# Four graph layers on one core: norms inside their loops, long VectorE operations cut up, the sorted list loaded without a meeting

## The chip, the cores and the metric

The kernel runs on one core of a Trainium2 chip. The core has five engines with a queue each: PE (TensorE), DVE (VectorE), ACT (ScalarE), POOL (GpSimd) and SP (SyncE, which issues transfers). The metric is the device time of one execution in microseconds, lower is better; the time before is the median of three runs.

## The reference

Four graph layers, each on `relu(layernorm(x))`, each added to `x` (3125 nodes of 64 values, 53125 edges with random ends):

```python
# layer 0: sum, maximum and mean of the edges' 32 attributes by source node, then a dense layer
h = jnp.concatenate([seg_sum, seg_max, seg_mean, u[batch]], axis=1)
h = jax.nn.relu(h @ W1 + b1) @ W2 + b2
# layer 1: attention with 8 heads over edges and self loops, softmax by destination node
logits = jax.nn.leaky_relu(a_src[src] + a_dst[dst], negative_slope=0.2)
out = jax.ops.segment_sum(h[src] * alpha[:, :, None], dst, num_segments=n).mean(axis=1) + bias
# layer 2: messages of edge, sender and receiver, mean by destination node, then an update
h = jax.nn.silu(msg_in @ W1_msg + b1_msg)
node_messages = _segment_mean(h @ W2_msg + b2_msg, receivers, node_emb.shape[0])
new = jax.nn.silu(concat([node_emb, node_messages]) @ W1_upd + b1_upd) @ W2_upd + b2_upd
# layer 3: signed cosine similarity of Wh at the two ends, weighted sums by source node
prop_pos = jax.ops.segment_sum((base * sim_pos)[:, None] * Wc, row, num_segments=n_nodes)
```

## The kernel before, in words

Nodes lie in 25 tiles of 128 (`x` and `hn` are 128 partitions x 25 x 64). Each tile group (`GROUPS`) has four tiles, 256 columns of `x`, but for the last, with one tile. A list of 56320 entries (edges, one entry per node, padding) lies as 128 partitions x 440. What a layer needs of its entries' other ends POOL gathers with indirect DMAs, one for each of the 440 columns: 128 rows of a table in HBM. There are five such lists of gathers: the edge records of layer 0 (L838), the edge rows in destination order (L1284, L1303, L1312), and the tables of layers 1, 2 and 3 (L792); and three times 25 gathers for the node sums (L968, L2388, L2761).

`sort_sources` sorts the entries by source node on DVE. Meanwhile PE and ACT make the edge rows of layer 2: 55 units of a product (`project`) and a copy (`keep`), and after each fifth unit ACT issues a store of 1320 KB (L584). When the sort is done, SP stores the keys (L352) and waits, all engines meet (`Step`), SP loads the keys back in another shape (L640), DVE masks the entry's index out of them (L666), and POOL, which waits for `indexed` (L834), begins layer 0's gathers.

While POOL gathers, DVE sorts by destination and makes layer 0's sums. `collect` turns them into node sums: `sel` (L1006) compares 3200 columns at once. POOL's 25 gathers of node sums are followed by early edge gathers (`early_edges`). `layer0_finish` then makes the features, a dense layer in a loop over the groups (`node_dense`: PE transposes, ACT copies, PE, ACT, PE, DVE adds), the norm over all 25 tiles at once (`normalise`), and the table of layer 1, which SP stores; SP raises `renewed` (L1247), for which POOL waits before layer 1's gathers. The bias of layer 1 is added in `layer1_spread` (L1698), that of layer 2 in `layer2_weights` (L2160), each with one operation of 1600 columns.

`layer2_tail` works in a loop over the seven groups, in which the engines' stages are shifted against each other. For a group: the average on DVE (L2541, L2543), transposes on PE (L2429), a copy on ACT (L2491), a product (L2438), DVE's join with the node's own part (L2567), SiLU on ACT (L2498), a second product (L2447), and on DVE the addition to `x` and the centring and squares of the norm (L2549 to L2559), two rounds later. What is carried over from the partition before comes in by products on PE (`carries`, L2413), the third set of them before group 2. After the loop follow one square root, seven norms of two operations each (L2577, L2579), the products for layer 3 (L2460, L2469) and seven pieces of its table on DVE (L2583 to L2588), each stored by two transfers (L2396, L2397). POOL begins layer 3's gathers when all fourteen have landed.

## Time and profile before

| | us |
|---|---|
| median of the three runs (3107.81 to 3112.47) | 3111.59 |
| profiled execution, its own time | 3117.0 |
| span of the profiled execution | 3115.1 |
| POOL busy (71% of the span, 2299 instructions) | 2197.5 |
| DVE busy (42%) | 1320.8 |
| PE busy (20%) | 608.3 |
| ACT busy (15%) | 481.4 |

The shares are of the span. POOL has issue time of 0.30 us between two gathers that doesn't count as busy. Line numbers are those of the kernel before; SPq and ACTq are the transfers that SyncE and ScalarE issue.

### The profile page before, as it was taken

The page shows a single profiled execution, that of the slowest core. Times are in us where ns is not written, and L with a number is a line of the kernel's source. Part 1 is how long each engine was busy: PE and PEld are TensorE (multiplying, and loading weights), DVE is VectorE, ACT ScalarE, POOL GpSimd, SP SyncE. Part 2 cuts the span into 40 slices and gives each one's busy share as a digit, 9 for nine tenths or more (in the row PEclk, how much of TensorE's full clock was granted, in tenths as well). Part 3 has the DMA queues.
Part 4 walks back from the last instruction along what each step waited for, and adds up shares of the span by engine and source line. Part 5 has one row for each costly group of instructions (what it writes and reads, how often), then busy time and mean ns, then how long its engine had stood idle before and what let it go on. Part 6 is the DMA issues. An engine that isn't in the chain of part 4 may idle for free.

```text
span 3115.1 us, 14443 instructions
## 1 busy us (share of the span) xinstructions
PE 608.3 (20%) x3300; PEld 468.3 (15%) x3301; DVE 1320.8 (42%) x1909; ACT 481.4 (15%) x447; POOL 2197.5 (71%) x2299
## 2 busy tenths in 40 slices
PE   5421130001500000001888850000000400000001
PEld 5411110001300000001666640000000300000001
DVE  8788885202310000009466643243344505353455
ACT  2200006211100000000000022222223211211220
POOL 0177777777777777777777777777777367777774
PEclk8665565555555555555899975555555555555555
DMA  9311115212355756755455424333333222323232
GB/s 321 113 25 15 14 27 92 70 33 62 65 52 52 65 59 59 64 52 65 110 135 150 108 51 74 108 90 128 91 117 91 42 55 72 90 72 91 72 88 53
DMA packets 195586, 248.87 MB, mean 80 GB/s; under 512 B 138820, under 2 KB 149694, under 8 KB 187975
## 3 DMA queue, kind: packets, MB, share of 16 engines
q0 software_dynamic: 74048, 114.24, 20.2%
q1 hardware_dynamic: 63414, 104.50, 10.5%
q10 hardware_dynamic: 58064, 29.51, 8.5%
q14 instruction: 45, 0.36, 0.0%
q8 instruction: 15, 0.25, 0.0%
HBM read 154.17 MB, written 93.93 MB: 80 GB/s over the span
## 4 chain that ended last, share of the span: by engine, by line
POOL 55%; issue 19%; DVE 2%; ACT 0%; DMA 0%; DVEq 0%; POOLq 0%; ACTq 0%
POOL l1g_rows L792 13%; POOL l2g_rows L792 13%; POOL l3g_rows L792 12%; POOL ep_rows L1303 11%; POOL ep_rows L1284 2%; POOL l2t_res L2388 1%; POOL l0f_res L968 1%; POOL l3t_res L2761 1%; DVE l3g_banks L2708 0%; DVE l3g_banks L2732 0%; ACT l3g_banks L2666 0%; DVE l3g_banks L2729 0%; DVE l3g_dot L2715 0%; DVEq L2714 0%; POOL ep_rows L1312 0%
## 5 line engine op out<-in xcount | busy, mean ns | idle before, releaser
L838 POOL DMA_INDIRECT l0g_rows<-in_rec_s,ents x440 | 427.3, 971 | 139.8 <-issue 133.8
L792 POOL DMA_INDIRECT l2g_rows<-tab,ep_rows x440 | 417.6, 949 | 134.2 <-issue 134.2
L792 POOL DMA_INDIRECT l1g_rows<-tab,srct x440 | 416.9, 948 | 134.1 <-issue 134.1
L792 POOL DMA_INDIRECT l3g_rows<-tab,others x440 | 416.1, 946 | 134.2 <-issue 134.2
L1303 POOL DMA_INDIRECT ep_rows<-recp,entd x352 | 339.9, 966 | 107.3 <-issue 107.3
L1505 DVE TENSOR_TENSOR l1s_A<-l1s_bank,l1s_mk 110x512 f32<-110x512 f32 x8 | 5.3, 688 | 533.6 <-PE l1s_bank L1467 533.6
L1763 PE MATMUL l1a_pa<-l1a_g,l1a_wt 128*128 x1296 | 169.2, 290 | 0.0
L1763 PEld LDWEIGHTS l1a_pa<-l1a_g,l1a_wt 128*128 128x128 f32 x1296 | 158.7, 202 | 24.3 <-issue 24.3
L2328 DVE COPY l2g_mix<-l2g_q 128x64 f32<-128x64 f32 x11 | 2.5, 228 | 308.1 <-ACT l2g_mix L2289 308.1
L2706 DVE COPY l3g_banks<-l3g_q 128x65 f32<-128x65 f32 x12 | 2.7, 229 | 306.9 <-ACT l3g_banks L2666 306.6
L1467 PE MATMUL l1s_bank<-ident,atp 128*110 128x128 f32 x64 | 11.4, 357 | 544.5 <-ACT atp L1406 535.6
L2767 PE MATMUL l3t_nmp<-ident,l3t_nmb 128*64 128x128 f32 x2 | 0.7, 448 | 585.3 <-DVEq L2784 585.3
L1284 POOL DMA_INDIRECT ep_rows<-recp,entd x82 | 83.2, 1015 | 25.0 <-issue 24.7
L1779 DVE TENSOR_TENSOR l1a_wt<-l1a_place,item_ex 128x1536 f32<-128x1536 f32 x54 | 94.9, 1758 | 7.7
L302 POOL IOTA iot<- 128x3200 f32 x1 | 2.8, 2803 | 132.8 <-DVE sorts_raw L316 132.8
L1406 ACT COPY atp<-l1g_rows 128x704 f32 (+1 forms) x10 | 8.3, 827 | 554.8 <-DMA l1g_rows<-tab,srct 554.8
L1467 PEld LDWEIGHTS l1s_bank<-ident,atp 128*110 128x110 f32 x64 | 10.9, 218 | 545.2 <-issue 536.1
L2666 ACT COPY l3g_banks<-l3g_rows 128x2860 f32<-128x2860 f32 (+3 forms) x12 | 55.2, 4599 | 221.0 <-DMA l3g_rows<-tab,others 221.0
L2767 PEld LDWEIGHTS l3t_nmp<-ident,l3t_nmb 128*64 128x64 f32 x2 | 0.3, 204 | 585.4 <-DVEq L2784 585.4
L390 DVE TENSOR_TENSOR sortd_x<-sortd_x 128x512 f32<-128x512 f32 (+1 forms) x128 | 85.6, 669 | 4.2
L391 DVE TENSOR_TENSOR sortd_x<-sortd_x 128x512 f32<-128x512 f32 (+1 forms) x128 | 84.5, 660 | 0.0
L1787 DVE TENSOR_TENSOR acc<-acc,l1a_pa 128x780 f32 x54 | 52.3, 968 | 74.4 <-PE l1a_pa L1767 74.4
(580 smaller groups left out, 2320.7 us busy)
## 6 DMA issues: line engine op xcount, KB each, us to landing
l1a_g<-g SPq DMA_DIRECT2D x54, 390.0 KB
recp<-ep_rows ACTq DMA_DIRECT2D x11, 1320.0 KB, 7.5
g<-l1g_rows ACTq DMA_DIRECT2D x10, 1430.0 KB, 25.4
sums<-l0s_sums SPq DMA_DIRECT2D x10, 1408.0 KB, 5.1
sums<-l2o_sums SPq DMA_DIRECT2D x9, 1408.0 KB, 5.0
sums<-l3o_sums SPq DMA_DIRECT2D x9, 1408.0 KB, 5.4
rowsd<-ep_rows POOLq DMA_DIRECT2D x8, 1452.0 KB, 6.4
ep_rows<-rowsd SPq DMA_DIRECT2D x8, 1452.0 KB, 6.6
```

The source lines that it names most:

```text
L390: v.tensor_tensor(out[0], pair[0], pair[1], ALU.min).then_inc(step, 1)
L391: v.tensor_tensor(out[1], pair[0], pair[1], ALU.max).then_inc(step, 1)
L792: nc.gpsimd.indirect_dma_start(out=ring.rows[:, s, j, :], out_offset=None, in_=table, in_offset=bass.IndirectOffsetOnAxis(ap=index(b, s, j ...
L838: nc.gpsimd.indirect_dma_start(out=rows[:, j, :], out_offset=None, in_=K.a["rec_s"], in_offset=bass.IndirectOffsetOnAxis(ap=K.by_src.ent[: ...
L968: nc.gpsimd.indirect_dma_start(out=res[:, w, :], out_offset=None, in_=table, in_offset=bass.IndirectOffsetOnAxis(ap=end[:, w:w + 1], axis= ...
L1284: nc.gpsimd.indirect_dma_start(out=ring.rows[:, s, j, :], out_offset=None, in_=K.recp, in_offset=bass.IndirectOffsetOnAxis(ap=K.by_dst.ent ...
L1303: nc.gpsimd.indirect_dma_start(out=ring.rows[:, s, j, :], out_offset=None, in_=K.recp, in_offset=bass.IndirectOffsetOnAxis(ap=K.by_dst.ent ...
L1763: nc.tensor.matmul(pa[b][:, bass.ds(places[u], P)], wt[:, b, u].rearrange("p h s -> p (h s)"), g[:, b, bass.ds(slots[u], P)], start=False, ...
L1779: v.tensor_tensor(wt[:, b], place[:, b].unsqueeze(2).to_broadcast([P, IB, H, WIN]), K.item_ex[:, :, bass.ds(n * IB, IB)].rearrange("p h i ...
L1787: v.tensor_tensor(sums, sums, used[b], ALU.add).then_inc(added, 1)
L2388: nc.gpsimd.indirect_dma_start(out=res[:, w, :], out_offset=None, in_=K.sums2, in_offset=bass.IndirectOffsetOnAxis(ap=by.end[:, w:w + 1], ...
L2666: nc.scalar.copy(cut(bank_of(i), C1, n)[:, :, 1:], ring.rows[:, b % RING, c0:c0 + n, C1:].rearrange("p j f -> p f j")).then_inc(spread, 1)
```

## The change

**Start.** The buffers of the list's keys live in a phase of their own. SP issues the loads of the keys directly behind its wait for their store; DVE masks the index in the same step; the meeting at the step's end no longer includes POOL. ACT keeps its last unit back until the keys are loaded, and POOL waits for ACT's end of the units (`edges.done`) beside `indexed`.

**Long operations.** The operations of 1600 and 800 columns in `collect`, `layer0_finish`, `layer1_spread` and `layer2_weights`, and `sel` in `collect` are cut into groups of four tiles or thirds. `sel` in `layer2_tail` and layer 3's finish are as they were.

**Layer 0's norm.** The centring and the squares are made for each group inside the dense layer's loop on DVE. The square root follows after the loop; the scaling and the maximum are one operation for each group.

**Layer 2's finish.** A group goes through both products in its own round on PE and ACT, except that the last two go together; on DVE the centring comes one round after the average. The norm's scaling and maximum are one operation, and the table pieces start after four norms, with a norm between each two.

```diff
             K.rows = EdgeRows(ph)
-            sort_sources(K)
-
-            layer0_pass(K)
+            with Phase(K, "first") as first:
+                K.first = FirstList(first)
+                sort_sources(K)
+                layer0_pass(K)
...
-        with Step(nc) as block:
+        key, nxt, prv = K.first.key, K.first.nxt, K.first.prv
+        keyed, clean = ph.sems("keyed", "clean")
+
+        with Step(nc, pool_ahead=True) as block:
...
+                dve.wait_ge(keyed, 16)
+                v.tensor_scalar(K.by_src.ent[:, :], key[:, :], 0xFFFF, None, ALU.bitwise_and).then_inc(K.by_src.indexed, 1)
...
                     for i in units_after(m):
+                        if i == UNITS - 1:
+                            act.wait_ge(keyed, 16)
                         edges.keep(nc, act, i, K.recp)
+                edges.finish(act)
...
                 sp.wait_ge(stored, 48)
+                sp.dma_start(key[:, :], K.by_src.key[0:L].rearrange("(p j) -> p j", p=P)).then_inc(keyed, 16)
+                sp.wait_ge(clean, 1)
+                with nc.allow_non_contiguous_dma(reason="one value per partition"):
+                    sp.dma_start(nxt[:, :], K.by_src.key[J:J + L].rearrange("(p j) -> p j", p=P)[:, 0:1]).then_inc(K.first.loaded, 16)
...
+    def finish(self, act):
+        act.wait_ge(self.kept, UNITS)
+        act.sem_inc(self.done, 1)
...
             def _(pool):
+                pool.wait_ge(K.edges.done, 1)
                 pool.wait_ge(K.by_src.indexed, 1)
...
-                v.tensor_scalar(sel[:, :], K.iot[:, :], fk[:, 0:1], None, ALU.is_equal)
+                for w, n in GROUPS:
+                    ws = slice(w * P, (w + n) * P)
+                    v.tensor_scalar(sel[:, ws], K.iot[:, ws], fk[:, 0:1], None, ALU.is_equal)
...
+                    for w, n in THIRDS:
+                        ws = slice(w, w + n)
+                        v.tensor_tensor(tmp[:, ws, nsum:D], tmp[:, ws, nsum:D], has[:, ws].unsqueeze(2).to_broadcast([P, n, D - nsum]),
+                                        ALU.add)
...
                     put(nc.vector, slice(w, w + n), pc[t % 2][:, 0:n * C].rearrange("p (w c) -> p w c", c=C)).then_inc(used, 1)
+                    if after is not None:
+                        nc.vector.drain()
+                        after(nc.vector, slice(w, w + n), n)
...
+    def centre(self, v, ws, n):
+        x, hn, mean, var, sq = self.K.x, self.K.hn, self.mean, self.var, self.sq
+        v.tensor_reduce(mean[:, ws], x[:, ws, :], AX.X, ALU.add)
+        v.drain()
+        v.tensor_scalar(mean[:, ws], mean[:, ws], 1.0 / D, None, ALU.mult)
+        v.drain()
+        v.tensor_tensor(hn[:, ws, :], x[:, ws, :], self.wide(mean, ws, n), ALU.subtract)
+        v.drain()
+        v.tensor_tensor(sq[:, ws, :], hn[:, ws, :], hn[:, ws, :], ALU.mult)
+        v.drain()
+        v.tensor_reduce(var[:, ws], sq[:, ws, :], AX.X, ALU.add)
...
-                v.tensor_tensor(K.hn[:, :, :], K.hn[:, :, :], wide(var), ALU.mult)
-                v.drain()
-                v.tensor_scalar(K.hn[:, :, :], K.hn[:, :, :], 0.0, None, ALU.max)
+                for w, n in GROUPS:
+                    ws = slice(w, w + n)
+                    v.scalar_tensor_tensor(hn[:, ws, :], hn[:, ws, :], 0.0, self.wide(var, ws, n), ALU.max, ALU.mult)
...
-        node_dense(K, "l0m", feat, 97, K.a["L0_gnn_W1"], 128, ACT.Relu, K.a["L0_gnn_b1"], K.a["L0_gnn_W2"], put, pool_ahead=True)
-    normalise(K, "n1", True)
+        node_dense(K, "l0m", feat, 97, K.a["L0_gnn_W1"], 128, ACT.Relu, K.a["L0_gnn_b1"], K.a["L0_gnn_W2"], put, pool_ahead=True,
+                   after=norm.centre)
+        norm.finish(K)
...
-                v.tensor_tensor(K.x[:, :, :], K.x[:, :, :], T.bias[:, :].unsqueeze(1).to_broadcast([P, NT, D]), ALU.add)
+                for w, n in GROUPS:
+                    v.tensor_tensor(K.x[:, w:w + n, :], K.x[:, w:w + n, :], T.bias[:, :].unsqueeze(1).to_broadcast([P, n, D]), ALU.add)
...
+                for t in range(NG - 2):
+                    average(t)
+                    if t:
+                        centre(t - 1)
+                    join(t)
+                average(NG - 2)
+                centre(NG - 3)
+                average(NG - 1)
+                join(NG - 2)
+                join(NG - 1)
+                centre(NG - 2)
+                centre(NG - 1)
...
-                for w, n in GROUPS:
+                def norm(t):
+                    w, n = GROUPS[t]
                     ws = slice(w, w + n)
-                    v.tensor_tensor(K.hn[:, ws, :], K.hn[:, ws, :], wide(var, ws, n), ALU.mult)
-                    v.drain()
-                    v.tensor_scalar(K.hn[:, ws, :], K.hn[:, ws, :], 0.0, None, ALU.max).then_inc(normed, 1)
+                    v.scalar_tensor_tensor(K.hn[:, ws, :], K.hn[:, ws, :], 0.0, wide(var, ws, n), ALU.max, ALU.mult).then_inc(normed, 1)
...
+                for t in range(NG + NORMED):
+                    if t < NG:
+                        norm(t)
+                    if t >= NORMED:
+                        table(t - NORMED)
```

The order of PE's instructions in layer 2's loop before, from the first transposes (`l2t_a` the transposed averages, `l2t_b` the first product, `l2t_c` the second, `l2t_carried` the carries):

```order
L2429 MATMUL l2t_a<-ident,l2t_res 128x128 x4
L2438 MATMUL l2t_b<-l2t_at,l2o_Wr 128x256
L2413 MATMUL l2t_carried<-l2t_car,l2t_sel 128x64 x8
L2429 MATMUL l2t_a<-ident,l2t_res 128x128 x2
L2438 MATMUL l2t_b<-l2t_at,l2o_Wr 128x256
L2447 MATMUL l2t_c<-l2o_W,l2t_ht 128x128 x2
L2429 MATMUL l2t_a<-ident,l2t_res 128x128 x2
L2438 MATMUL l2t_b<-l2t_at,l2o_Wr 128x256
```

The same place now:

```order
L2493 MATMUL l2t_a<-ident,l2t_res 128x128 x2
L2498 MATMUL l2t_b<-l2t_at,l2o_Wr 128x256
L2507 MATMUL l2t_c<-l2o_W,l2t_ht 128x128 x2
L2493 MATMUL l2t_a<-ident,l2t_res 128x128 x2
L2498 MATMUL l2t_b<-l2t_at,l2o_Wr 128x256
L2507 MATMUL l2t_c<-l2o_W,l2t_ht 128x128 x2
L2480 MATMUL l2t_carried<-l2t_car,l2t_sel 128x64 x8
L2493 MATMUL l2t_a<-ident,l2t_res 128x128 x2
```

The second product of a group now comes in the group's own round, and the third set of carries stands behind group 1's second product, where it stood between two stages of group 1 and 0.

DVE in layer 0's finish before, from the loop's additions to layer 1's table (`x` the nodes, `hn` the normed nodes, `n_` the norm's buffers):

```order
L1203 TENSOR_TENSOR x<-x,l0m_c 128x256 x6
L1203 TENSOR_TENSOR x<-x,l0m_c 128x64
L1140 TENSOR_REDUCE n_mean<-x 128x25
L1142 TENSOR_SCALAR n_mean<-n_mean 128x25
L1144 TENSOR_TENSOR hn<-x,n_mean 128x1600
L1146 TENSOR_TENSOR n_sq<-hn 128x1600
L1148 TENSOR_REDUCE n_var<-n_sq 128x25
L1150 TENSOR_SCALAR n_var<-n_var 128x25
```

The beginning of the same place now:

```order
L1266 TENSOR_TENSOR x<-x,l0m_c 128x256
L1190 TENSOR_REDUCE l0f_mean<-x 128x4
L1192 TENSOR_SCALAR l0f_mean<-l0f_mean 128x4
L1194 TENSOR_TENSOR hn<-x,l0f_mean 128x256
L1196 TENSOR_TENSOR l0f_sq<-hn 128x256
L1198 TENSOR_REDUCE l0f_var<-l0f_sq 128x4
L1266 TENSOR_TENSOR x<-x,l0m_c 128x256
```

Five operations of the norm have moved between each two additions of the loop, each on 256 columns at a time.

DVE at the table of layer 3 now, after the loop of layer 2 (`wh` the table's pieces):

```order
L2668 SCALAR_TENSOR_TENSOR hn<-hn,l2t_var 128x256 x4
L2674 TENSOR_TENSOR wh<-l2t_b,l2o_b 128x4x64
L2677 TENSOR_TENSOR l2t_sq<-wh 128x256
L2679 TENSOR_REDUCE wh<-l2t_sq 128x4
L2668 SCALAR_TENSOR_TENSOR hn<-hn,l2t_var 128x256
L2674 TENSOR_TENSOR wh<-l2t_b,l2o_b 128x4x64
```

Before, all fourteen norm operations stood ahead of the first piece.

## Rows read from the trace of the kernel before

**Rows 1.** The page's part 4: the chain that ended last, shares by engine
```profile
POOL 55%; issue 19%; DVE 2%; ACT 0%; DMA 0%; DVEq 0%; POOLq 0%; ACTq 0%
```

**Rows 2.** Timeline at the start: start us, us, engine, line, operation [idle before]
```profile
135.91 0.33 ACTq L584 DMA_DIRECT2D recp<-ep_rows  x1
136.55 0.34 SPq L352 DMA_DIRECT2D keys<-sorts_raw  x1
...
144.05 0.39 DVE L666 TENSOR_SCALAR ents<-sets_key 128x440 int32<-128x440 int32 x1 [1.47 <-DMA sets_key<-keys]
...
145.41 1.13 POOL L838 DMA_INDIRECT l0g_rows<-in_rec_s,ents  x1 [6.01 <-DVE ents L666]
```

**Rows 3.** Waits of SyncE's queue: us in total, times, longest
```profile
SPq L354 <- DMA keys<-sorts_raw: 4.2, 1, 4.2
```

**Rows 4.** Transfers: issues, KB each, us to landing
```profile
pairs<-sortd_node SPq DMA_DIRECT2D x1, 256.0 KB, 2.2
```

**Rows 5.** Timeline in layer 0's finish: gathers beside long operations
```profile
735.62 2.56 POOL L968 DMA_INDIRECT l0f_res<-sums,ends  x1 [0.31 <-issue]
...
806.59 1.82 DVE L1144 TENSOR_TENSOR hn<-x,n_mean 128x1600 f32<-128x1600 f32 x1
806.81 2.42 POOL L1284 DMA_INDIRECT ep_rows<-recp,entd  x1 [0.30 <-issue]
```

**Rows 6.** A stretch of layer 0's finish: us, POOL busy (count), clock, DMA
```profile
776.00:816.00 40.00, 31.58 (x28) 0.67 0.17 27
```

**Rows 7.** Timeline from the dense loop to the last early gather
```profile
794.02 0.42 DVE L1203 TENSOR_TENSOR x<-x,l0m_c 128x256 f32<-128x256 f32 x1 [10.84 <-PE l0m_c L1097]
...
804.25 1.28 ACT L1162 ACT_TABLE_LOAD   x1 [1.24 <-ACTq L218]
...
812.53 0.23 ACT L1162 ACTIVATE n_var<-n_var 128x25 f32<-128x25 f32 x1 [7.00 <-DVEq L1151]
...
846.72 0.94 POOL L1284 DMA_INDIRECT ep_rows<-recp,entd  x1 [0.30 <-issue]
```

**Rows 8.** The line that raises `renewed`: duration ns, start us
```profile
L1247 SPq EVENT_SEMAPHORE  x1: 17/17/17, 845.9 to 845.9; - x1
```

**Rows 9.** Timeline around layer 1's finish: POOL's gathers
```profile
1493.33 3.02 POOL L1303 DMA_INDIRECT ep_rows<-recp,entd  x1 [0.30 <-issue]
...
1858.58 0.95 POOL L1303 DMA_INDIRECT ep_rows<-recp,entd  x1 [0.30 <-issue]
...
1880.39 1.89 POOL L792 DMA_INDIRECT l2g_rows<-tab,ep_rows  x1 [0.30 <-issue]
```

**Rows 10.** Waits of SyncE's queue between 1850 and 1870
```profile
SPq L1868 <- DMA tab<-l1f_tab: 1.4, 1, 1.4
```

**Rows 11.** Timeline of layer 2's finish
```profile
2439.77 3.52 PE L2413 MATMUL l2t_carried<-l2t_car,l2t_sel 128*128 128x64 f32 x16
...
2447.93 0.41 DVE L2549 TENSOR_TENSOR x<-x,l2t_c 128x256 f32<-128x256 f32 x1
...
2450.66 0.42 DVE L2567 TENSOR_TENSOR l2t_both<-l2t_b,wh 128x256 f32<-128x256 f32 x1
...
2472.42 0.43 DVE L2577 TENSOR_TENSOR hn<-hn,l2t_var 128x256 f32<-128x256 f32 x1
2472.92 0.29 DVE L2579 TENSOR_SCALAR hn<-hn 128x256 f32<-128x256 f32 x1
...
2474.49 1.22 PE L2469 MATMUL l2t_b<-l2o_W,l2t_ft 128*128 128x128 f32 x4
...
2477.06 0.42 DVE L2583 TENSOR_TENSOR wh<-l2t_b,l2o_b 128x256 f32<-128x256 f32 x1
...
2479.17 0.37 SPq L2396 DMA_DIRECT2D tab<-wh  x1
...
2501.91 0.95 POOL L2637 DMA_INDIRECT l3g_first<-tab,node0ns  x1 [45.04 <-issue]
```

**Rows 12.** Two us of the stores: PE, PEld, DVE, ACT, POOL busy, clock, DMA, GB/s
```profile
2488.00:2490.00 2.00, 0.00 (x0) 0.00 (x0) 0.00 (x0) 0.00 (x0) 0.00 (x0) 0.50 1.24 154
```

More of the change, by code:

```diff
@@ L63 @@
 NG = len(GROUPS)
+THIRDS = [(w, min(9, NT - w)) for w in range(0, NT, 9)]
 PAIRS = [(2 * i, min(2, NT - 2 * i)) for i in range((NT + 1) // 2)]
@@ L630, in list_setup @@
         groups = [(w, min(3, NT - w)) for w in range(0, NT, 3)]
-        pairs = by is K.by_dst
         if not pairs:
-            by.indexed = ph.sem("indexed")
+            loaded = K.first.loaded
         ent = ph.sb("bit", [P, J], I32) if pairs else by.ent
-        kd = K.pairs if pairs else by.key
+        kd = K.pairs
         keep, after, node0, fk, nm = by.keep, by.after, by.node0, by.fk, by.nm
@@ L653, in _ @@
                 v = nc.vector
[L654 removed]
+                if pairs:
+                    v.memset(prv[:, :], 0).then_inc(blank, 1)
+                else:
+                    dve.wait_ge(K.first.ranked, 1)
                 v.memset(shift[:, :, :], 0.0)
@@ new lines, in expand @@
+                def expand(u):
+                    m, rows = pairs_of(GROUPS[u])
+                    pe.wait_ge(acted, u + 1)
+                    if u >= 2:
+                        pe.wait_ge(added, u - 1)
+                    for k in range(m):
+                        lt = nc.tensor.matmul(pc[u % 2][:, k * P:k * P + rows], ht[0:rows, u % 2, k * P:(k + 1) * P],
+                                              T.W2[0:rows, 0:rows], start=True, stop=True)
+                    lt.then_inc(second, 1)
@@ new lines, in average, with join @@
+                def average(t):
+                    w, n = GROUPS[t]
+                    ws = slice(w, w + n)
+                    dve.wait_ge(kept, min(4, (w + n - 1) // 8 + 1))
+                    dve.wait_ge(got[t], n * 16)
+                    v.tensor_tensor(res[:, ws, :], res[:, ws, :], carried[:, ws, :], ALU.add)
+                    v.drain()
+                    v.tensor_tensor(res[:, ws, :], res[:, ws, :], wide(T.r, ws, n), ALU.mult).then_inc(averaged, 1)
+                def join(u):
+                    w, n = GROUPS[u]
+                    m, rows = pairs_of(GROUPS[u])
+                    dve.wait_ge(first, u + 1)
+                    if u >= 2:
+                        dve.wait_ge(acted, u - 1)
+                    v.tensor_tensor(both[0:rows, u % 2, 0:m * P], pb[u % 2][0:rows, 0:m * P],
+                                    T.own[0:rows, w * D:w * D + m * P], ALU.add).then_inc(joined, 1)
@@ L2569, in _ @@
+                for t in range(NG - 2):
+                    average(t)
[9 more added lines that the diff above has]
+                centre(NG - 1)
                 v.drain()
```

246 lines of the change are left out of this document (120 added, 126 removed).

## The prediction, as it was put on record

> **What bounds the kernel now.** I read the page's chain first, then the timeline of GpSimd (POOL) for its gaps and for gathers that take too long, then the other engines around each. The chain lies on POOL's gathers from 145 us on [rows 1]. A gather is 0.95 us busy and 0.30 us issue, so one starts every 1.25 us [rows 9], more than 2,200 times. That count doesn't change. POOL's queue therefore sets the time in all stages except four places: the wait for the sorted source list at the start [rows 2], the hand-over of layer 0's table to layer 1's gathers, that of layer 1's table to layer 2's [rows 9, 10], and layer 2's finish, after which layer 3's gathers begin at 2501.91 [rows 11]. A saved microsecond counts where POOL itself is late; where POOL then meets a table that is not yet stored, it counts only up to that table.
>
> **Start.** The key store is issued at 136.55, right behind the last edge block's store of 1320 KB at 135.91 [rows 2]. SyncE then waits 4.2 us, so it lands at 136.55 + 0.34 + 4.2 = 141.1 [rows 3]. A store of the same 256 KB with nothing ahead of it lands in 2.2 us [rows 4]. From 141.1 to the first gather at 145.41 are 4.3 us: the meeting (about 0.3), the load of the keys, the mask (0.39) and 0.97 until POOL starts [rows 2]. The change keeps ScalarE's last unit back until the keys are loaded, so the 1320 KB are no longer ahead: the store lands at 136.55 + 2.2 = 138.75. It takes the meeting away, but adds a wait of POOL for ScalarE: last copy about 0.6, as its others, and issue of the block's store 0.33 [rows 2], about 1.0 us after the keys, against 0.39 for the mask beside it, so 0.6 more. First gather: 138.75 + 4.3 - 0.3 + 0.6 = 143.35, **-2.1 us**. Behind ScalarE's wait are only that store and the meeting; the store then has until the edge gathers at 707. Bounds: -0.3, if the store takes as long without the block; -2.6, if the wait for ScalarE costs nothing.
>
> **Long VectorE operations.** Gathers beside a long VectorE operation are stretched: 2.56 beside the comparison of 3200 columns, 2.42 beside a 1.82 us tensor_tensor of 1600 [rows 5]. The first delays the node sums on which all of layer 0's finish waits, so it is wholly on the path: 2.56 - 0.95 = **-1.6** (at least -1.0, if the pieces of 512 still hold POOL a little). The Trainium skill, "SBUF — State Buffer", section "Who interferes with whom", says that a two-port tensor_scalar locks GpSimd out and infers that a tensor_tensor doesn't keep it from making descriptors. The comparison's row agrees; the tensor_tensor's row speaks against the inference, and the row decides.
>
> Between 776 and 816 POOL is busy 31.58 us in 28 gathers [rows 6]: 31.58 - 28 x 0.95 = 5.0 us of stretching, which the pieces take away. But is POOL late there? Its last early gather ends at 846.72 + 0.94 = 847.66 [rows 7], and the table is stored at 845.9 [rows 8]: POOL has only 1.75 us to gain. And the table gets later. Between VectorE's first addition, 794.02, and the square root at 812.53 [rows 7] stood PE's loop and then the norm; now each group's centring stands in the loop. One such centring, from the addition to the next step, is 2450.66 - 2447.93 = 2.73 us in layer 2, beside running gathers [rows 11]. Six groups and a last one of a quarter width (about 1.75): 794.02 + 6 x 2.73 + 1.75 = 812.15. So the loop isn't faster than the separate norm. After it the meeting, and only then ScalarE loads its table, 1.28 us, which before ran from 804.25 under the norm's operations [rows 7]: root at about 813.6, +1.1. The fused pieces then cost 7 x 0.35 = 2.4 us against some 2.8 (-0.4). Ahead of the loop an addition of 1600 goes from 1.82 to at most 6 x 0.41 + 0.2 = 2.7 [rows 5, 11], and five operations of 800 into thirds; I take +0.7 for all. The table comes 1.4 later after the node sums, at 847.3; POOL waits for it and starts again about 0.3 after, at 847.6 against 847.66. **0.0** for this whole part (-1.4 if the table isn't later; +1.6 if it is 3 us later). What is late next is the table, not POOL.
>
> Layer 1's bias: one gather takes 3.02 [rows 9], 2.07 too many. But POOL ends there at 1858.58 + 0.95 = 1859.53, and layer 1's table has landed only about 0.1 earlier: its last store was issued at 1857.98, and SyncE's wait was 1.4 [rows 10]. POOL will arrive 2 us sooner and wait: **0.0** (up to +0.3 for being woken). Layer 2's bias lies under a gather of 1.89 [rows 9], with 400 gathers behind it and no wait among them: **-0.9** (at least -0.5).
>
> **Layer 2's finish.** After 2501.91 everything hangs on POOL, which waits for the last table store. In 2488 to 2490 the stores move 154 GB/s with a DMA share of 1.24 and no engine busy [rows 12]: from the first store at 2479.17 [rows 11] the stage is bound by the transfer of 2.5 MB, so its end moves with the first store. Two parts move that one.
>
> (a) From the first norm operation at 2472.42 to the first store are 6.75 us, because seven norms come before the first table piece at 2477.06. Group 0's product was started at 2474.49 and ready 0.6 later, at 2475.1 [rows 11]. With the fused operation (0.43 instead of 2472.92 + 0.29 - 2472.42 = 0.79) it is ready 0.36 sooner, 2.3 us after the first norm. Four fused norms end before that, so the table piece begins at 2.3 instead of 4.64: **-2.3**. Pieces then follow each other more slowly, as a norm stands between them, but under 2.1 us against 3 of transfer for each group.
>
> (b) The loop before. Now a group goes through product, join, SiLU and second product in its own round, and only two centrings stand behind the last group's average instead of three and a half: in the best case 3.9 us. But the round is now a closed chain: join 0.4, SiLU 0.5, product 1.1, centring 2.65 and signals make 4.8 us, against 4 x 1.25 = 5.0 for the next four gathers. And the 16 carry products of 3.5 us [rows 11], which had stood where PE waited anyway, now stand between group 1's last and group 2's first product. My replay by these durations (it gives 2471.7 for the end of the loop before, where the trace has 2471.5) puts group 2's join at 2449.1, 2.2 late, and this is regained by only 0.2 a group; the two last groups end at 2470.6. **-1.0** (0 to -3.9).
>
> **Sum.** -2.1 - 1.6 + 0 + 0 - 0.9 - 2.3 - 1.0 = -7.9 us. The profiled execution took 3117.0 (span 3115.1 and 1.9 around it), so 3109.1 for its like; it lies 5.4 above the median of the three runs, 3111.6, and against that I predict **3103.7**.
>
> **Rivals.** (A) Layer 2's loop doesn't fall behind, since the carries come out of the way (PE at its higher clock, or arrivals later than I think): (b) gives 3.9. For it: PE is free most of the loop. Against it: program order puts the carries on the chain. 3103.7 - 2.9 = 3100.8.
> (B) Less comes off: the key store isn't held by the block (-0.3 at the start) and the loop (b) gives nothing: 3103.7 + 1.8 + 1.0 = 3106.5, and with layer 0's table at its late bound 3108.1. For it: three hand-overs are within 2 us of the next bound.
> (C) Slower: layer 0's table decides. Its loop now issues 42 VectorE operations while POOL gathers; if each had to wait for half a gather, 0.47 us, that is 42 x 0.47 = 19.7 us more before the table, all of it on POOL's path: 3103.7 + 19.7 = 3123.4. It ends above the time before as soon as the table comes 8 us later than I have it, 1.1 a group. Against it: 2.73 for the same operations beside gathers [rows 11].
> (D) The skill's inference holds, that tensor_tensor doesn't stretch gathers, and something else beside it did: then layer 2's bias gives nothing, 3104.6. Against it: [rows 5, 9].
>
> **How the numbers follow.** My forecast has 0.50, A 0.18, B 0.21, C 0.07, D 0.04. Best bounds together: -2.6 - 1.6 - 1.4 - 0.9 - 6.2 = -12.7, 3098.9; worst without C: -0.3 - 1.0 + 1.6 + 0.3 - 0.5 - 1.3 = -1.2, 3110.4. With the runs' own spread the range is 3098 to 3111. What this measurement can tell from no change is 0.2%, 6.2 us. Faster by more: 0.40 of my forecast, all of A, 0.03 of D, 0.61. Within it: 0.10, B, 0.01, 0.02 of C, 0.34. Slower: 0.05.
>
> **What would show it.** First gather near 143.4, with ScalarE's last copy just before it. No gather over 1.3 us between the first node-sum gather and layer 1's table; POOL idle once, under 1 us, before layer 1's gathers and about 2 us before layer 2's. ScalarE's table load after layer 0's loop. In layer 2's finish the first table store about 4.4 us after the first norm, and the first norm about 1 us earlier against the node sums' gathers; layer 3's first gather 3.3 us earlier against them. It is wrong if the transfer's end doesn't move with its first store, or if POOL waits for layer 0's table by more than 2 us.

## The result, and the profile after

The changed kernel took 3105.39 us (median of 20 runs, 3101.48 to 3108.05), the kernel before 3111.53 (20 runs, 3107.81 to 3114.07): ratio 0.9981, interval 0.9974 to 0.9987, so 6.1 us faster. In a second pair of measurements it was 3099.89 against 3107.58 (7 and 11 runs), ratio 0.9971, interval 0.9960 to 0.9982. The forecast was 3103.7 us, between 3098 and 3111. The edited kernels below were all measured in series in which the kernel before, too, took 3944 to 3954 us (the long series; the recorded expectations speak of slow and fast calls), so their times are compared only with the kernel before in the same series.

The first two profiles say -11.3 us (spans 3115.1 and 3103.8). Each kernel was therefore profiled once more (3109.1 and 3101.0), and I split all four at POOL's gathers. The sort's end is counted from the start of its last operation on VectorE:

| stretch, us | before, two profiles | changed, two | mean | forecast |
|---|---|---|---|---|
| sort's end to first gather | 9.31, 9.52 | 6.98, 6.83 | -2.5 | -2.1 |
| to layer 0's first node-sum gather | 589.0, 589.5 | 588.5, 590.2 | +0.1 | 0 |
| from there to layer 1's first gather | 114.2, 114.2 | 112.1, 113.1 | -1.6 | -1.6 |
| to layer 2's first | 1011.3, 1011.2 | 1012.0, 1008.5 | -0.9 | 0 |
| to its first node-sum gather | 564.4, 563.8 | 563.0, 562.4 | -1.4 | -0.9 |
| to the first norm operation | 48.23, 48.33 | 48.61, 48.62 | +0.3 | -1.0 |
| to the first table store | 6.75, 6.75 | 5.08, 5.07 | -1.7 | -2.3 |
| to layer 3's first gather | 22.74, 19.56 | 20.16, 20.43 | -0.9 | 0 |
| to its first node-sum gather | 569.7, 569.5 | 570.3, 569.1 | +0.1 | 0 |

The five stretches with a forecast gain sum to -6.9 (forecast -7.9), beside -6.1 and -7.7 by the medians. The row of the stores differs as much between two profiles of one kernel as between the kernels, and so does the time to the sort's end (136.1 and 133.5 before, 133.8 and 134.0 changed): chance, as far as four profiles can tell. The row of layer 1 is partly a gain: in the second profile of the changed kernel POOL didn't wait for the table at all (below).

The chain that ended last, by engine, has POOL's gathers as before. The shares are not to be compared with [rows 1]: the chain of the kernel before was followed back only to 731.5 us (its shares sum to 76%), this one to the start. So [rows 1] doesn't show a chain "from 145 us on", as the prediction reads it; in the second profile of the kernel before the chain does reach layer 0's gathers (POOL 69%).

```profile
POOL 69%; issue 24%; DVE 5%; DMA 1%; PE 1%; ACT 1%; DVEq 0%; POOLq 0%; ACTq 0%
```

The start in the changed kernel's timeline (start us, us, engine, line, operation, idle before), which answers to [rows 2]:

```profile
133.79 0.43 DVE L333 TENSOR_SCALAR sorts_raw<-sorts_x 128x512 int32<-128x512 int32 x1
134.24 0.34 SPq L374 DMA_DIRECT2D keys<-sorts_raw  x1
...
136.27 0.33 SPq L376 DMA_DIRECT2D first_key<-keys  x1
...
138.77 0.59 ACT L608 COPY ep_rows<-sorts_proj 128x512 f32<-128x512 f32 x1 [5.68 <-DMA first_key<-keys]
138.77 0.39 DVE L335 TENSOR_SCALAR ents<-first_key 128x440 int32<-128x440 int32 x1 [4.55 <-DMA first_key<-keys]
139.39 0.33 ACTq L612 DMA_DIRECT2D recp<-ep_rows  x1
...
140.77 1.10 POOL L876 DMA_INDIRECT l0g_rows<-in_rec_s,ents  x1 [3.67 <-ACTq L617]
```

And the wait of SyncE's queue there, which answer to [rows 3]:

```profile
SPq L376 <- DMA keys<-sorts_raw: 1.7, 1, 1.7
```

The key store lands 0.34 + 1.7 us after its start, where it took 0.34 + 4.2. The block's store comes only at 139.39, and POOL is released last by ScalarE.

Layer 0's finish, against [rows 5, 7, 8]: the gathers beside the cut comparison, the first addition of the loop, ScalarE's table load and root, POOL's last early gather and its wait.

```profile
730.52 1.30 POOL L1006 DMA_INDIRECT l0f_res<-sums,ends  x1 [0.30 <-issue]
732.13 1.18 POOL L1006 DMA_INDIRECT l0f_res<-sums,ends  x1 [0.30 <-issue]
...
789.11 0.42 DVE L1266 TENSOR_TENSOR x<-x,l0m_c 128x256 f32<-128x256 f32 x1 [10.83 <-PE l0m_c L1142]
...
806.93 1.28 ACT L1219 ACT_TABLE_LOAD   x1 [8.83 <-ACTq L221]
808.22 0.23 ACT L1219 ACTIVATE l0f_var<-l0f_var 128x25 f32<-128x25 f32 x1
...
836.18 0.94 POOL L1349 DMA_INDIRECT ep_rows<-recp,entd  x1 [0.30 <-issue]
840.43 0.59 POOL L1330 DMA_DIRECT2D rowsd<-ep_rows  x1 [3.31 <-SPq L1312]
```

At the border of layers 1 and 2 ([rows 9] before), in the first profile of the changed kernel and then in its second one (t1):

```profile
1853.35 0.94 POOL L2281 DMA_INDIRECT l2g_first<-tab,node0nd  x1 [2.59 <-DMA tab<-l1f_tab]
```

```profile
1852.57 0.94 POOL L2281 DMA_INDIRECT l2g_first<-tab,node0nd  x1 [0.30 <-issue]
```

Beside the cut bias of layer 2, again in the first profile:

```profile
1873.14 2.24 DVE L2227 TENSOR_TENSOR x<-x,l2o_b2u 128x256 f32<-128x256 f32 x7 [6.78 <-DMA l2o_b2m<-in_L_gnn_b_msg]
1873.44 0.95 POOL L829 DMA_INDIRECT l2g_rows<-tab,ep_rows  x1 [0.30 <-issue]
1874.69 1.04 POOL L829 DMA_INDIRECT l2g_rows<-tab,ep_rows  x1 [0.30 <-issue]
```

Layer 2's finish before, the join of group 0, which [rows 11] doesn't show:

```profile
2440.02 0.42 DVE L2567 TENSOR_TENSOR l2t_both<-l2t_b,wh 128x256 f32<-128x256 f32 x1 [1.64 <-PE l2t_b L2438]
```

And changed, against [rows 11]: the joins of groups 0, 1 and 2, with the carries between the last two, the first norm, the product for the table, its first piece, its first store, layer 3's first gather.

```profile
2429.06 0.42 DVE L2627 TENSOR_TENSOR l2t_both<-l2t_b,wh 128x256 f32<-128x256 f32 x1 [4.04 <-PE l2t_b L2498]
...
2433.96 0.41 DVE L2627 TENSOR_TENSOR l2t_both<-l2t_b,wh 128x256 f32<-128x256 f32 x1
...
2435.98 3.51 PE L2480 MATMUL l2t_carried<-l2t_car,l2t_sel 128*128 128x64 f32 x16
...
2441.76 0.42 DVE L2627 TENSOR_TENSOR l2t_both<-l2t_b,wh 128x256 f32<-128x256 f32 x1 [2.52 <-PE l2t_b L2498]
...
2464.99 1.43 DVE L2668 SCALAR_TENSOR_TENSOR hn<-hn,l2t_var 128x256 f32<-128x256 f32 x4
...
2466.69 1.23 PE L2539 MATMUL l2t_b<-l2o_W,l2t_ft 128*128 128x128 f32 x4
...
2467.95 0.42 DVE L2674 TENSOR_TENSOR wh<-l2t_b,l2o_b 128x256 f32<-128x256 f32 x1 [1.52 <-PE l2t_b L2539]
...
2470.07 0.37 SPq L2463 DMA_DIRECT2D tab<-wh  x1
...
2490.23 0.95 POOL L2734 DMA_INDIRECT l3g_first<-tab,node0ns  x1 [41.47 <-issue]
```

From one join to the next are 4.9 us (2429.06 to 2433.96), but 7.8 across the carries. From group 0's join to the first norm are 35.9 us, where it was 32.4 (2440.02 to 2472.42). Behind the four norms VectorE waits 1.52 us for the first product of the table.

### The profile page after: what moved, and what is told of

It reads as the page before. It is cut to its first block, busy times and chain, and to the rows that moved or that the text cites. A ratio compares the mean times of both kernels' runs of the same rounds, so it can differ in the third digit from the quotient of the medians.

```text
span 3103.8 us, 14533 instructions
## 1 busy us (share of the span) xinstructions
PE 612.8 (20%) x3300; PEld 468.7 (15%) x3301; DVE 1325.8 (43%) x1977; ACT 481.9 (16%) x447; POOL 2188.3 (71%) x2299
## 4 chain that ended last, share of the span: by engine, by line
POOL 69%; issue 24%; DVE 5%; DMA 1%; PE 1%; ACT 1%; DVEq 0%; POOLq 0%; ACTq 0%
POOL l0g_rows L876 14%; POOL l1g_rows L829 13%; POOL l2g_rows L829 13%; POOL l3g_rows L829 12%; POOL ep_rows L1368 11%; POOL ep_rows L1349 3%; DVE sorts_x L418 1%; DVE sorts_x L419 1%; POOL l2t_res L2455 1%; POOL l3t_res L2858 1%; POOL l0f_res L1006 1%; PE sorts_proj L593 0%; DMA recp<-ep_rows 0%; DVE l3g_banks L2805 0%; DVE l3g_banks L2829 0%
## 6 DMA issues: line engine op xcount, KB each, us to landing
g<-l1g_rows ACTq DMA_DIRECT2D x10, 1430.0 KB, 22.3
```

## The experiments

All edited kernels were measured in long series, on a chip (among others) that also gave 3110 us for the kernel before. Their stretches are compared with those above only where POOL isn't gathering or where they are the same in both kinds of series. In block_not_held VectorE has 36 pauses of 5 to 36 us for which the profile shows no wait ("issue"), 618 us in all, 98% of it while POOL gathers; in the four profiles of the normal series it has none over 5 us. In layer 2's finish the waits of VectorE and then of ScalarE are these (us in total, times, longest; "remote" is a signal whose sender isn't in the profile):

```profile
DVE l2t_res L2615 <- issue: 25.9, 1, 25.9
DVE l2t_both L2625 <- PE l2t_b L2496: 25.4, 3, 21.6
```

```profile
ACT l2t_carried L2546 <- remote: 51.2, 2, 30.7
```

Not every pause ends with the gathers: ScalarE's second one here ends at 3217.81, 17 us after the end of layer 2's last node-sum gather (3200.85), and between 3205 and 3217 no engine and no transfer of the core is busy. From the first join at 3219.98 on there are no more such pauses, and all data of the loop are there. That made a clean measurement of it.

**Block not held (a1).** Its edit:

```diff
-                        if i == UNITS - 1:
-                            act.wait_ge(keyed, 16)
```

> The changed kernel, but ScalarE's last unit isn't kept back until the keys are loaded, so the last edge block's store of 1320 KB goes out just before the key store, as before. Measured from the last operation of the sort on VectorE (the mask into the raw keys) to POOL's first gather: 9.31 us before, 6.98 in the changed kernel. My theory (the block's transfer is what held the key store): SyncE waits about 4.2 us for the key store again instead of 1.7, ScalarE's last copy no longer stands behind the keys (-0.6), so the distance is 6.98 + 2.5 - 0.6 = 8.9 and the time 1.9 us above the changed kernel's, other things equal. Rival (the meeting and the keys' load behind it were the cost, the block's store is nothing): the key store lands as soon as now, the distance is 6.4 and the time 0.6 below the changed kernel's.

3950.52 us, ratio to before 1.0012 (1.0003 to 1.0021). From sort's end to first gather 8.19 us. The keys' store went out 0.76 us ahead of the block's this time and wasn't held (SyncE waited 1.7 us for it); it was the keys' load that took longer beside the block:

```profile
133.84 0.34 SPq L372 DMA_DIRECT2D keys<-sorts_raw  x1
...
134.60 0.33 ACTq L610 DMA_DIRECT2D recp<-ep_rows  x1
135.88 0.33 SPq L374 DMA_DIRECT2D first_key<-keys  x1
...
140.22 0.39 DVE L335 TENSOR_SCALAR ents<-first_key 128x440 int32<-128x440 int32 x1 [6.41 <-DMA first_key<-keys]
...
141.58 1.15 POOL L874 DMA_INDIRECT l0g_rows<-in_rec_s,ents  x1 [4.88 <-DVE ents L335]
```

The block costs something (1.2 us here, 2.25 in s1 below, where the theory had 1.9); that it must be the store that waits doesn't hold. The rival's 6.4 is out.

**Norm outside (a2, and q3 in another series).** `after=norm.centre` goes, and `finish` begins with

```diff
+                self.centre(v, slice(0, NT), NT)
```

> The changed kernel, but layer 0's centring and squares stand behind the dense loop again, over all 25 tiles at once in operations of 1600 columns (the scaling stays cut and fused). From the first node-sum gather to the raising of the semaphore for layer 1's table: 111.5 us before, 110.8 in the changed kernel, whose POOL then waited 3.3 us. My theory (the norm in the loop doesn't bring the table sooner, it only frees gathers, which had no one waiting): table at most 0.6 us sooner, gathers stretched by about 4 us, so that POOL ends about 0 to 1 us behind the table; layer 1's first gather within 1 us of the changed kernel's. Rival (the norm in the loop is worth something on the table's path): table and first gather of layer 1 later by 2 us or more, and the time with it.

> The changed kernel, but layer 0's centring and squares stand behind the dense loop again, over all 25 tiles at once in operations of 1600 columns (the scaling stays cut and fused). From the first node-sum gather to layer 1's first gather: 114.2 us in both profiles of before, 112.05 in the changed kernel, where POOL waits 3.3 us for the table. Theory (the norm in the loop doesn't bring the table sooner): the table up to 0.6 us sooner, gathers stretched by about 4 us, so that POOL ends within 1 us of the table; the distance is 111.5 to 112.8 and the time within 0.8 us of the changed kernel's. Rival (the norm in the loop is what brought the 2.15 us): 114.

3951.05 and 3959.42 us, ratios 1.0011 (1.0002 to 1.0020) and 1.0013 (1.0004 to 1.0022). From layer 0's first node-sum gather to layer 1's first are 171.9 and 172.4 us (172.1 in s1), and 168.7 to 170.5 in five kernels with the norm in the loop (a1, a3, a4, q1, q4). Pauses and 60 us of POOL's waiting lie in these, so the question (the table against the early gathers) is left without an answer here. The 1.4 to 3.7 us are no measure of it: with pauses in it the loop takes 24 to 29 us from its first to its last addition with the norm inside and 26.4 without (q4, whose other operations are whole, has 43.7), where the normal series have 16.0 and 17.3 with it and 9.8 without.

What can be read is the end. From the loop's last addition to the square root of the norm are 8.6 us with the norm outside (8.7 and 8.9 before) and 3.1 with it inside, in both kinds of series. So in the normal series the norm inside takes 5.6 to 5.7 us off behind the loop and puts 6.2 and 7.5 into it: the root comes 19.1 and 20.5 us after the first addition, where it came 18.5 and 18.7 after it.

**Old loop in layer 2 (a3, and q1 in another series).** The three loops of PE, ScalarE and VectorE as before; on VectorE:

```diff
+                for t in range(NG + 3):
+                    if t < NG:
+                        average(t)
+                    if t >= 3:
+                        centre(t - 3)
+                    if 1 <= t <= NG:
+                        join(t - 1)
```

> The changed kernel, but layer 2's loop in the order of before (stages of the groups shifted against each other on PE, ScalarE and VectorE), with the fused norm and the early table pieces kept. From POOL's first node-sum gather of layer 2 to the first norm operation: 48.24 us before, 48.61 in the changed kernel; from there to the first table store 6.75 and 5.08. Theory after the result (the new order of the loop brings nothing, as the carries' 3.5 us stand on its chain and the round of 4.9 us doesn't catch up): the first norm 0.0 to 0.6 us sooner than in the changed kernel, first store still 5.1 behind it, time 0 to 0.6 us less. Rival (my prediction's term, -1.0): first norm 1.0 us later and the time with it.

> The changed kernel, but layer 2's loop in the order of before on PE, ScalarE and VectorE; the fused norm and the early table pieces are kept. From POOL's first node-sum gather of layer 2 to the first norm operation: 48.2 and 48.4 us in two profiles of before, 48.6 in the changed kernel. Theory (the new order brings nothing, as the carries' 3.5 us stand on its chain and its round of 4.9 us can't catch up): 48.2 to 48.4 here, the first store still 5.1 behind it, the time 0 to 0.5 us below the changed kernel's. Rival (my prediction's term of -1.0): first norm at 49.4, the time 0.8 above.

3940.70 and 3949.95 us: ratios 0.9987 (0.9978 to 0.9996) and 0.9990 (0.9981 to 0.9999). The first norm stands 79.4 and 79.6 us after the first node-sum gather, and 87.6 to 87.8 in the four kernels of the long series with the changed loop and its carries (a1, a2, q3, q4): the changed order loses 8 us here. VectorE's first and last join and the first norm, in the old order (a3):

```profile
3223.06 0.42 DVE L2617 TENSOR_TENSOR l2t_both<-l2t_b,wh 128x256 f32<-128x256 f32 x1 [20.77 <-PE l2t_b L2505]
...
3245.39 0.27 DVE L2617 TENSOR_TENSOR l2t_both<-l2t_b,wh 64x128 f32<-64x128 f32 x1
3250.82 1.43 DVE L2653 SCALAR_TENSOR_TENSOR hn<-hn,l2t_var 128x256 f32<-128x256 f32 x4
```

and in the changed order (a1):

```profile
3219.98 0.42 DVE L2625 TENSOR_TENSOR l2t_both<-l2t_b,wh 128x256 f32<-128x256 f32 x1 [21.61 <-PE l2t_b L2496]
...
3249.48 0.28 DVE L2625 TENSOR_TENSOR l2t_both<-l2t_b,wh 64x128 f32<-64x128 f32 x1 [1.28 <-PE l2t_b L2496]
3255.88 1.43 DVE L2666 SCALAR_TENSOR_TENSOR hn<-hn,l2t_var 128x256 f32<-128x256 f32 x4
```

With all data there the old order needs 27.8 us from the first join to the norm, the changed one 35.9. With data arriving by gathers (the normal series) it is 32.4 and 32.3 for the old, 35.9 and again 35.9 for the changed order. So the changed loop never waits for the gathers: its own round is its limit, while the old one follows them (VectorE waits 1.0 to 4.7 us for them before each of the first six averages).

**Carries by group (a4, and in q2 and r1).**

```diff
-                    if t in CARRY_AT:
-                        carries(2 + CARRY_AT.index(t))
                     project(t)
+                    if t + 3 < NG:
+                        carries(t + 3)
                     expand(t)
```

> The changed kernel, with layer 2's carries made for one group at a time: those of groups 0 to 2 before the loop, then one set of 1.76 us between a group's first and second product, where PE waits 1.1 to 1.5 us anyway. Theory (the third set of 3.52 us on the chain costs 2.8 us and is never regained): group 2's join 22.6 us after the first node-sum gather instead of 25.4, first norm at 46.4 instead of 48.6, the time 2 us less. Rival (the closed round of join, SiLU, product and centring decides, and 1.76 us in it cost as much as the block did): the first norm within 0.5 us of the changed kernel's or later.

3945.25 us, ratio 0.9999 (0.9990 to 1.0008). From first join to norm 33.56 us instead of 35.9: 2.3 us of the expected 2.8. The three rounds that carry a set of 1.76 us take 5.2, 5.2 and 4.9, so a little of it shows. The rival (first norm no sooner) is out.

**The kernel before again (p0).** No edit.

> The kernel before once more, for a second profile of it. In its first profile the sort's last operation stood at 136.10 us, in the changed kernel's at 133.79, with the difference in one wait of VectorE for ScalarE's turned blocks (4.37 us against 2.30); and its layer 3 stores took 22.7 us from the first store to POOL's next gather against 20.2. If both are chance, this profile has the sort's end at 133 to 134 and the stores near 20 us; if they are the kernel's own, 136 and 22.7 again. From the sort's last operation to the first gather 9.3 us in either case. The four runs before this one were on a chip where all engines but POOL have long pauses without a wait while POOL gathers (3946 us for the kernel before, against 3112); if it is that chip again, only the start can be compared.

3110.22 us beside 3110.19 for the same kernel. Sort's end at 133.52, the stores' stretch 19.56, first gather 9.52 after the sort's end: both odd values of the first profile were chance.

**Three edits (q2; r1 is the same kernel measured again).** Carries by group, and

```diff
+                if spare is not None:
+                    nc.scalar.sqrt(spare, K.ident[:, 0:1])
...
+            if i == UNITS - 1:
+                act.sem_inc(self.done, 1)
+                act.wait_ge(keyed, 16)
             act.dma_start(table.rearrange("(p j) d -> p j d", p=P)[:, b * EB:(b + 1) * EB, :],
```

> The changed kernel with three edits, each read in a stretch of its own. (1) Layer 2's carries are made for one group at a time: groups 0 to 2 before the loop, then one set of 1.76 us between a group's first and second product, where PE waits 1.1 to 1.5 us anyway. Theory (the set of 3.52 us on the chain costs 2.8 us and isn't regained): from the first node-sum gather to group 2's join 22.6 us instead of 25.4, to the first norm 46.4 instead of 48.6. Rival (the closed round of join, SiLU, product and centring decides): first norm at 48.1 or later. (2) ScalarE takes one square root of a spare value behind the last activation of layer 0's dense loop, so that its table is loaded under the norm's operations. Theory (layer 0's table decides when layer 1's gathers begin, POOL waited 3.3 us for it): from the first node-sum gather to layer 1's first gather 110.9 instead of 112.05. Rival: ScalarE's table doesn't stand on the path, 112. (3) ScalarE's last unit isn't kept back, only its store is; POOL is released before that store is issued. Theory: from the sort's end to the first gather 6.4 instead of 6.98; rival: VectorE's mask then decides only 0.1 later, 6.9. Sum by the theories -4.0: 3101.4 us where the changed kernel has 3105.4; by the rivals 3105.

> The same kernel as q2 (carries by group, ScalarE's table load under the norm, only the last store kept back), in a call of its own: the two calls of four kernels gave 3946 to 3959 us for every kernel, the one with a single kernel 3110 for the kernel before, on the same chip. In the slow calls its start was 6.36 us (theory 6.4) and its first norm of layer 2 3.4 us sooner than in kernels with the changed loop. Theories here: first norm 46.4 us after the first node-sum gather (changed kernel 48.6), layer 1's first gather 110.9 after layer 0's first node-sum gather (112.05), start 6.4 (6.98): -4.0 in all, 3101.4 us. Rival: the round of layer 2's loop decides in this state (first norm 48.1 or later) and layer 0's table isn't the limit (112): 3104.7.

3954.35 and 3944.59 us, ratios 1.0002 (0.9993 to 1.0011) and 0.9995 (0.9986 to 1.0004): no difference from before in these series. By stretches: sort's end to first gather 6.36 us in both (6.98 and 6.83 changed), as expected; first join to norm 33.57 and 33.55; from the last addition of layer 0's loop to the root 2.23 us instead of 3.14 (forecast a gain of 1.15). ScalarE's timeline in r1:

```profile
1080.25 1.28 ACT L1161 ACT_TABLE_LOAD   x1
1081.55 0.20 ACT L1161 ACTIVATE l0f_spare<-ident 128x1 f32<-128x1 f32 x1
1087.72 0.23 ACT L1217 ACTIVATE l0f_var<-l0f_var 128x25 f32<-128x25 f32 x1 [5.97 <-DVEq L1206]
```

The load now lies under the loop's last operations, worth 0.9 us on the table's path. The three sum to 0.5 + 0.9 + 2.4, about 3.8 us; carried over to the normal series this would be 3101.6 us, an estimate, as these edits were not measured in one.

**Long operations whole (q4).** `GROUPS` and `THIRDS` in the cut operations become one piece of all 25 tiles.

> The changed kernel, but the long operations whole again as before (the comparison of 3200 columns in layer 0, those of 800 and 1600 columns in layer 0's finish, the biases of layers 1 and 2); the norm stays in its loop, cut. Theory: the node-sum gathers take 1.0 us longer (2.56 instead of 1.30 and 1.18), layer 0's finish is 0.7 us shorter for the whole operations, the gathers beside the biases of layers 1 and 2 take 3.0 and 1.9 us again, and of these only the last is on the path: 1.0 - 0.7 + 0.9 = 1.2 us above the changed kernel. Rival (every stretched gather counts): 1.0 + 4 + 1.4 + 0.9, 7 us above. Second rival, from the Trainium skill, which infers that a tensor_tensor doesn't hold up GpSimd's descriptors: the gathers beside the two biases take 0.95 to 1.3 us.

3957.16 us, ratio 1.0009 (1.0000 to 1.0018). The time can't tell 1.2 from 7 us here, but the gathers beside the biases can be read. Layer 2's bias, and POOL beside it:

```profile
2590.50 1.82 DVE L2227 TENSOR_TENSOR x<-x,l2o_b2u 128x1600 f32<-128x1600 f32 x1 [6.86 <-DMA l2o_b2m<-in_L_gnn_b_msg]
2590.69 2.44 POOL L829 DMA_INDIRECT l2g_rows<-tab,ep_rows  x1 [0.30 <-issue]
```

In s1 it is 2.46. Cut, as shown above, the same place has 0.95 and 1.04. The gather beside layer 1's whole bias takes 2.01 here. So the second rival is out: a tensor_tensor of 1600 columns did hold a gather up in each of these places. Between the theory and the first rival nothing is decided.

**Four parts undone (s1).** Block not held, norm outside, biases whole, old loop.

> The changed kernel with four parts undone, each read in its own stretch (changed kernel's value in brackets). (1) The last unit isn't kept back: from the sort's end to the first gather 8.2 us as in the slow call (6.98), since there the keys' load, not their store, met the block's store. (2) Layer 0's centring behind the loop over all 25 tiles: from the first node-sum gather to layer 1's first gather (112.05). Theory (the loop's norm brings the table no sooner, gathers stretch by 4 us but POOL had 3.3 us to wait): 111.5 to 112.8. Rival (the norm in the loop brought the 2.15 us against before): 114. (3) The biases of layers 1 and 2 whole: gathers of 3.0 and 1.9 us again beside them; from layer 1's first gather to layer 2's no change (1012.0; theory: POOL waits for the table there), from there to layer 2's node sums +0.9 (563.1). By the Trainium skill's inference that a tensor_tensor doesn't hold up GpSimd's descriptors both gathers take under 1.3 us. (4) Layer 2's loop in the order of before: first norm 48.2 to 48.4 us after the first node-sum gather (48.6); by my prediction's term 49.6. All this holds if the call is one of the fast kind (about 3110 us for the kernel before); then the time is 3105.4 + 1.2 + 0.4 + 0.9 - 0.3 = 3107.6 us. In the slow kind (about 3946) VectorE is late everywhere and only (1) can be read.

3942.74 us, ratio 0.9996 (0.9985 to 1.0007): this too was a long series, so only the start, the loop and the gathers beside the biases can be read. Start 9.23 us, more than expected, since here the block's store (133.62) and the keys' (133.60) went out together and the keys' landed only 4.5 us later. So without the hold the start is 8.2 or 9.2, depending on which of the two transfers meets the block; with it, 6.8 to 7.1 in eight profiles. First join to norm 28.0, as in a3.

**The changed kernel again (t1).** No edit.

> The changed kernel itself, in a call of its own, as the missing base of the nine runs of other kernels, which all fell in calls of the slow kind (about 3946 us for the kernel before). If the call is of the fast kind: 3105.4 us against 3110 to 3111.5, first norm of layer 2 48.6 us after its first node-sum gather, layer 1's first gather 112.0 after layer 0's first node-sum gather, layer 3's stores between 19.6 and 22.7 us by chance. If it is of the slow kind: from the edited kernels (carries by group worth -2.8 on the way to the first norm, norm in the loop -3, start 7.0) the first norm stands at 87.6 after the first node-sum gather, layer 1's first gather 169 after layer 0's first node-sum gather, start 7.0, and the time is 1.0005 to 1.0009 of before: the old order of layer 2's loop, 8.1 us shorter here, makes the change a small loss. Rival: the edits' differences are chance between calls, and the ratio is 0.998 as in the fast kind.

3099.89 us, ratio 0.9971, in a normal series: its stretches are the second values for the changed kernel in the table. What the changed kernel takes in a long series wasn't measured. From a1, less its 1.2 us of start, it would be 3949.3 against 3945.8, 3.5 us above before: an estimate.

## Why the prediction was right, and where it wasn't

The time was forecast 1.7 us too low and its direction right. Part of the agreement is luck: of the terms, the start and layer 2's bias gave 0.4 and 0.5 us more than forecast, the two parts of layer 2's finish 0.6 and 1.3 less, and one of these has the wrong sign.

**Start: right.** Forecast -2.1, measured -2.5. The reason holds too: s1 has neither the hold nor the meeting and gives 9.23 us, before has 9.31 and 9.52, so the meeting was worth 0.1 to 0.3 (forecast 0.3). SyncE's wait for the keys' store went from 4.2, 4.6 and 4.5 us (before twice, s1) to 1.7, a gain of 2.5 to 2.9 (forecast 2.35), and POOL's wait for ScalarE costs 0.5 to 0.7 of that (r1: 6.36; forecast 0.6).

**Layer 0's comparison: -1.6 forecast, -1.2 measured** (node sums in hand 34.55 us after their first gather before, 33.5 and 33.2 now). The pieces still hold gathers a little, 1.30 and 1.18 in one profile and 1.25 in the other: between my bound of -1.0 and the term.

**Layer 0's norm: right in size, with a slip.** From the node sums in hand to the raised semaphore: 77.0 and 76.8 us before, 77.3 and 78.7 now, so the table comes 1.1 later on the mean (forecast 1.4). The ScalarE load is behind the loop as forecast. That the whole row is -1.6 as forecast comes of two deviations that cancel, the comparison's 0.4 and this 0.3. And the last section said POOL would wait under 1 us before layer 1's gathers, and that over 2 us would prove the account wrong. It waited 3.3 and 4.8. So one of the prediction's own signs of being wrong came true. My own numbers gave 4.6 (POOL 5.0 sooner, table about as late as POOL before): I had taken the gain on POOL's arrival for a wait. The sum wasn't touched, but the sign was set from the wrong number.

**Layer 1's bias: 0.0 forecast, right in one profile and not in the other.** The gather beside it went from 3.02 to 1.63 and 1.66, and POOL ended its edge gathers 1.5 and 2.7 us sooner after layer 1's first gather than before. In the first profile the table landed 2.3 us behind that and POOL waited 2.59 us in all (forecast about 2), so nothing was gained. In the second the table was there first, POOL didn't wait, and the stretch is 2.7 us shorter. My 0.0 took a table and a POOL that were 0.1 apart for a fixed order; the table's landing moved by 1.4 us between two profiles of the kernel before and by 3.7 between those of the changed one. What moves it isn't shown.

**Layer 2's bias: -0.9 forecast, -1.4 measured** by the whole stretch; 0.85 of it is the gather itself (1.89 to 1.04), the rest isn't assigned.

**Layer 2, (a): the mechanism right, the size off.** -2.3 forecast, -1.7 measured. The term mis-sized is the wait for group 0's first product: I took 0.6 us for it after the product's start, but it takes 1.22, and VectorE waits 1.52 before the first piece. I should have used the duration in [rows 11] itself.

**Layer 2, (b): wrong.** -1.0 forecast, +0.3 measured. The step that failed is the regain after the carries. I had group 2's join 24.9 us after the first gather (2449.1 less 2424.18), and measured are 25.4. Then I let the loop regain 0.2 a group, as a round of 4.8 against 5.0 of gathers. The round is 4.9, and 5.3 before group 5's join: nothing is regained, and that is 0.9 of the 1.3 us. What the runs put in its place is simpler: 35.9 us from first join to norm, whether data arrive or lie there. There is a gain at both ends, 3.2 to 3.3 us at the first join, which I hadn't named, and 2.9 of my best case of 3.9 behind the last average (from there to the norm 8.5 us are left of 11.4). About 6.4 us between were given back, 2.4 of them by the carries (a4). Rival A (the carries don't matter) is out; of B this half came true and the other, the start, did not, and the time lies between the forecast's and B's. C is out by the loop of layer 0, whose additions follow each other every 2.7 and 2.9 us on average (forecast 2.73). D is out by q4 and s1. In the worst sum of the prediction layer 2's finish stands at -1.3, and the prediction derives no such bound for it.

**The stores: not contradicted.** From the first store to layer 3's first gather are 22.7 and 19.6 us before, 20.2 and 20.4 now. That the end moves with the first store is seen only within this spread, which is as large as the gain it should carry. Eight profiles with the new order of the table pieces (all but those of one chip, last section) have 19.8 to 20.7, the second one of the kernel before 19.6, so a part of the 1.7 us may be lost again; that isn't shown.

## What to carry to other kernels

An order that closes each item's chain within a round shortens the ends of a loop but sets its rate by latency; sum the closed round with everything that stands in it, and compare it with the arrivals before counting the ends as gain. Where two things meet within a microsecond, look at a second profile before fixing which of them is late. Name for each wait which side is late now and by how much after all terms, since the same 5 us can be a gain or an idle engine. Where effects are 1 to 3 us, one profile of each kernel isn't enough: two of the same kernel differed by 6.0 us here.

## What the hardware showed that I had not expected

- The same program, the kernel before, took 3110 us or 3946 on one and the same chip (3944 to 3954 over all long series). In the long series engines pause for 5 us to tens of us without a wait that the profile shows, mostly while POOL gathers; with no gathers beside them the start (6.9 to 7.1 with the block held) and the way from the first norm to the store (5.08) are unchanged. No edited kernel was measured in a normal series, but the kernel before was just as long beside them, so it isn't the edits. The cause stays open.
- In layer 1's finish the same 16 products of 384 columns took 5.33 us in the first profile of the kernel before and 6.41 to 6.55 in the other three. The granted clock was at 0.98 to 1.00 (the 2.4 GHz level) all through them in the one and at 0.50 (1.2 GHz) for their first 2 us in the others, behind the same transposes (3.53 and 3.82 us long). From the start of these products to the table's last store were 23.1 us in the one and 24.1 to 24.2 in the others.
- The stores of layer 3's table took 22.3 to 23.0 us (from the first one to the next gather) in all four profiles of one chip, 19.6 to 20.7 in nine of the other ten, and 22.7 in the first of the kernel before.
